# Cross-attention kernel: the weighted sum accumulates in one PSUM bank, two banks by turns, and its division and rounding change engines

## The reference, cut to what matters

```
scores = einsum(Q, K) * scale          # per sentence: 16 heads x 56 queries = 896 rows, 1500 keys
attn   = softmax(scores)
out    = einsum(attn, V)               # the weighted sum
x      = x + out.reshape(...) @ Wo
```

## Time and profile before

| | |
|---|---|
| median of 3 runs | 4035.7 us (4034.22 to 4037.05) |
| the profiled execution, its own time | 4029.83 us |
| its span, first to last instruction | 4028.0 us |
| mean granted TensorE clock | 0.954 of full speed |
| VectorE / ScalarE / GpSimd busy | 78% / 66% / 63% |
| matmuls | 43467 |

### The profile page before, as it was taken

The page is one execution under the profiler, slowest core; times in us unless marked ns, Lnnn a source line. Parts: engine busy times, 40 slices in busy tenths (PEclk is TensorE's granted clock), DMA queues, the critical chain, the costliest instruction groups (busy, mean ns, idle before and its releaser), DMA issues.

```text
span 4028.0 us, 110585 instructions
## 1 busy us (share of the span) xinstructions
PE 3794.2 (94%) x43467; PEld 2887.3 (72%) x43467; DVE 3136.7 (78%) x6499; ACT 2673.5 (66%) x5365; POOL 2545.3 (63%) x2457
## 2 busy tenths in 40 slices
PE   6999999989979999999799999996997899999987
PEld 4777777766647777777577777775665677777765
DVE  6999999858888888887688887886654788888864
ACT  4887887756647777777377777772542577777752
POOL 4888888759856766677466766664001476676761
PEclk8999999979989999999699999997998899999998
DMA  5333333125432221221122122110000212222100
GB/s 130 104 110 111 112 107 109 41 90 159 142 111 57 60 61 54 60 61 43 28 60 61 54 61 61 54 56 19 3 1 18 65 54 64 57 58 63 55 22 15
DMA packets 157328, 266.80 MB, mean 66 GB/s; under 512 B 26632, under 2 KB 97432, under 8 KB 155432
## 3 DMA queue, kind: packets, MB, share of 16 engines
q1 hardware_dynamic: 156360, 259.67, 22.6%
q10 hardware_dynamic: 448, 0.06, 0.0%
HBM read 165.10 MB, written 50.26 MB: 53 GB/s over the span
## 4 chain that ended last, share of the span: by engine, by line
PE 87%; DVE 6%; POOL 2%; ACT 2%; DMA 1%; issue 1%; SPq 1%; POOLq 0%; DVEq 0%; ACTq 0%
PE ps L186 83%; PE ps L665 1%; DVE xn L166 1%; POOL wst L545 1%; PE ps L242 1%; DVE wst L823 1%; PE ps L255 1%; PE ps L1639 1%; DMA big<-big 1%; PE ps L1161 0%; DVE st L151 0%; DVE wst L778 0%; DVE relu L775 0%; ACT wb L324 0%; PE ps L193 0%
## 5 line engine op out<-in xcount | busy, mean ns | idle before, releaser
L545 POOL TENSOR_TENSOR wst<-wst 125x384 bf16<-125x384 f32 (+1 forms) x1536 | 1432.2, 932 | 833.1 <-ACT wst L751 772.3
L751 ACT ACTIVATE wst<-ps 125x448 f32<-125x448 f32 x3072 | 1518.1, 553 | 568.3 <-PE ps L186 553.8
L186 PE MATMUL ps<-big,cx 128*125 128x448 bf16 (+1 forms) x6144 | 1427.4, 353 | 0.7 <-DMA big<-topT 0.7
L186 PEld LDWEIGHTS ps<-cx,wst 125*128 125x128 bf16 x23040 | 1113.6, 98 | 307.5 <-POOL wst L545 15.2
L823 DVE TENSOR_TENSOR wst<-wst 125x512 bf16<-125x512 f32 (+1 forms) x1536 | 1270.2, 827 | 56.7 <-ACT wst L751 56.5
L186 PE MATMUL ps<-cx,wst 125*128 125x65 bf16 (+2 forms) x23040 | 1202.4, 204 | 12.1 <-POOL wst L545 11.6
L186 PEld LDWEIGHTS ps<-big,cx 128*125 128x125 bf16 (+1 forms) x6144 | 834.5, 137 | 283.9 <-issue 1.8
L186 PE MATMUL ps<-cx,big 128*128 128x500 bf16 (+1 forms) x2688 | 709.8, 317 | 10.2 <-DVE big L1744 2.6
L778 DVE TENSOR_REDUCE wst<-ps 128x1 f32<-128x500 f32 x896 | 604.5, 675 | 136.3 <-PE ps L186 123.6
L775 DVE CUSTOM_DVE_ANT_0 wst<-ps,wst 128x500 bf16<-128x500 f32 x448 | 302.9, 676 | 195.0 <-PE ps L186 150.5
L775 DVE CUSTOM_DVE_ANT_0 relu<-ps,relu 128x500 bf16<-128x500 f32 x448 | 302.1, 674 | 149.7 <-PE ps L186 81.4
(11 more groups left out here) (250 smaller groups left out, 4213.2 us busy)
## 6 DMA issues: line engine op xcount, KB each, us to landing
big<-big SPq DMA_DIRECT2D x768, 56.0 KB, 2.7
cx<-ctxT SPq DMA_DIRECT2D x96, 375.0 KB, 3.5
cx<-ctxN SPq DMA_DIRECT2D x64, 377.9 KB
cx<-in_ctxN SPq DMA_DIRECT2D x64, 375.0 KB
cx<-ctxT SPq DMA_DIRECT2D x96, 187.5 KB, 3.8
ctxN<-cx SPq DMA_DIRECT2D x32, 377.9 KB
ynN<-cx SPq DMA_DIRECT2D x32, 377.9 KB
cx<-ynN SPq DMA_DIRECT2D x32, 377.9 KB
```

What stands on the lines that cost most here:

```text
L186: return t.matmul(o, l, r, start=start, stop=stop, skip_group_check=True)
L545: g.tensor_tensor(pl[r][0:KP, at:], pf[r][0:KP, at:], pf[r][0:KP, at:].bitcast(BF16)[:, 1::2], ALU.subtract).then_inc(s["plp"], 1)
L751: e.activation(pf[T % 3][0:KP, cols], bank(2 + n2 % 3, 448)[0:KP], ACT.Exp, scale=scale).then_inc(s["ev"], 1)
```

## The change

The accumulator becomes one bank: the high weights times the low values are a matmul of their own that adds into the first 64 of a block's 65 columns. So a sentence needs 7 x 65 = 455 columns, and two banks (5 and 6) are used by turns. A step has 21 matmuls (7 x 65, 64, 65 columns). VectorE takes the reciprocal and multiplies straight out of PSUM into `raw`, ScalarE rounds from `raw` into `O`, and GpSimd only subtracts; the stage's last subtraction is VectorE's. TensorE waits for the accumulator of two sentences ago.

```diff
-        raw = [wst[:, 4032 + 903 * i:4935 + 903 * i].rearrange("p (j c) -> p j c", j=NJ) for i in range(2)]
+        raw = [wst[:, 4032 + 448 * i:4480 + 448 * i].rearrange("p (j c) -> p j c", j=NJ) for i in range(2)]
+        acc = [bank(5 + i, 65 * NJ) for i in range(2)]
...
# pool_cross
-                if 0 <= (k := due(T, KT + 4)) < B - 1:
-                    w.wait_ge(s["fc"], 2 * (kb + 1))
-                    g.tensor_tensor(r, r, raw[u][:, :, C + 1:], ALU.add).then_inc(s["fp"], 1)
...
-                if 0 <= (k := due(T, KT + 7)) < B - 1:
-                    w.wait_ge(s["rd"], kb + 1)
-                    g.tensor_tensor(r, r, per_row(rden[u][:, :], C), ALU.mult).then_inc(s["fp"], 1)
...
-                if 0 <= (k := due(T, KT + 8)) < B - 1:
-                    g.tensor_copy(O[:, k % HB, :, 0:C], r).then_inc(s["fp"], 1)
...
-                if 0 <= (k := due(T, KT + 10)) < B - 1:
-                    g.tensor_tensor(O[:, k % HB, :, C:], r, O[:, k % HB, :, 0:C], ALU.subtract).then_inc(s["fp"], 1)
+                if 0 <= (k := due(T, KT + 6)) < B - 1:
+                    kb = B * ci + k
+                    w.wait_ge(s["fp"], 2 * kb + 1)
+                    g.tensor_tensor(O[:, k % HB, :, C:], raw[k % 2], O[:, k % HB, :, 0:C], ALU.subtract).then_inc(s["fp"], 1)
+                    w.wait_ge(s["fp"], 2 * kb + 2)
+
+        def pe_values(t, w, ci, T):
+            k, i = divmod(T, KT)
+            r, kb = T % 3, B * ci + k
+            ph, o, of = pf[r][0:KP, :].bitcast(BF16)[:, 1::2], acc[k % 2], cnb[k % 3]
+            w.wait_ge(s["pl"], NT * ci + T + 1)
+            wait_values(w, ci, k)
+            if kb >= 2:
+                w.wait_ge(s["fc"], kb - 1)
+            for j in range(NJ):
+                if j == JP[ci]:
+                    w.wait_ge(s["plp"], NT * ci + T + 1)
+                cols, at = slice(128 * j, 128 * j + 128), 65 * j
+                mm(t, o[:, at:at + 65], ph[:, cols], of[:, i, 0:65], i == 0 and j == 0, False)
+                mm(t, o[:, at:at + 64], ph[:, cols], of[:, i, 65:129], False, False)
+                n = mm(t, o[:, at:at + 65], pl[r][0:KP, cols], of[:, i, 0:65], False, i == KT - 1)
+            n.then_inc(s["pv"], 1)
+
+        def dve_values(v, w, ci, k):
+            u, kb = k % 2, B * ci + k
+            o = acc[u].rearrange("p (j c) -> p j c", j=NJ)
+            w.wait_ge(s["pv"], KT * (kb + 1))
+            v.reciprocal(rden[u][:, :], o[:, :, C]).then_inc(s["rd"], 1)
+            if k >= 2:
+                w.wait_ge(s["fp"], 2 * (kb - 1))
+            w.wait_ge(s["rd"], kb + 1)
+            v.tensor_tensor(raw[u], o[:, :, 0:C], per_row(rden[u][:, :], C), ALU.mult).then_inc(s["fc"], 1)
+            if k == B - 1:
+                w.wait_ge(s["fp"], 2 * kb + 1)
+                v.tensor_tensor(O[:, k % HB, :, C:], raw[u], O[:, k % HB, :, 0:C], ALU.subtract).then_inc(s["fp"], 1)
+
+        def act_values(e, w, ci, k):
+            kb = B * ci + k
+            w.wait_ge(s["fc"], kb + 1)
+            w.wait_ge(s["fp"], 2 * kb)
+            if k >= HB:
+                w.wait_ge(s["otr"], kb - HB + 1)
+            e.activation(O[:, k % HB, :, 0:C], raw[k % 2], ACT.Copy).then_inc(s["fp"], 1)
...
# pe_cross: L634 to L653 become
+                    pe_values(t, w, ci, T - 2)
...
# act_cross: L724 to L731 become
+                if (k := due(T, KT + 4)) >= 0:
+                    act_values(e, w, ci, k)
...
# dve_cross: L800 to L815 go; after the subtraction of L823
+                if (k := due(T, KT + 2)) >= 0:
+                    dve_values(v, w, ci, k)
```

More of the change, by code:

```diff
@@ L547, in pool_cross @@
                     w.wait_ge(s["plp"], NT * ci + T)
-                if 0 <= (k := due(T, KT + 4)) < B - 1:
-                    u, kb = k % 2, B * ci + k
-                    r = raw[u][:, :, 0:C]
-                    w.wait_ge(s["fc"], 2 * (kb + 1))
-                    g.tensor_tensor(r, r, raw[u][:, :, C + 1:], ALU.add).then_inc(s["fp"], 1)
-                    w.wait_ge(s["fp"], 4 * kb + 1)
-                if 0 <= (k := due(T, KT + 7)) < B - 1:
-                    u, kb = k % 2, B * ci + k
-                    r = raw[u][:, :, 0:C]
-                    w.wait_ge(s["rd"], kb + 1)
-                    g.tensor_tensor(r, r, per_row(rden[u][:, :], C), ALU.mult).then_inc(s["fp"], 1)
-                    w.wait_ge(s["fp"], 4 * kb + 2)
@@ L560, in pool_cross @@
-                if 0 <= (k := due(T, KT + 8)) < B - 1:
[L561 to L564, removed]
-                    g.tensor_copy(O[:, k % HB, :, 0:C], r).then_inc(s["fp"], 1)
-                    w.wait_ge(s["fp"], 4 * kb + 3)
-                if 0 <= (k := due(T, KT + 10)) < B - 1:
-                    u, kb = k % 2, B * ci + k
-                    r = raw[u][:, :, 0:C]
-                    g.tensor_tensor(O[:, k % HB, :, C:], r, O[:, k % HB, :, 0:C], ALU.subtract).then_inc(s["fp"], 1)
-                    w.wait_ge(s["fp"], 4 * kb + 4)
+                if 0 <= (k := due(T, KT + 6)) < B - 1:
[3 more added lines that the diff above has]
+                    w.wait_ge(s["fp"], 2 * kb + 2)
@@ L662, in pe_cross @@
                 if what == "turn":
-                    w.wait_ge(s["fp"], 4 * (b0 + k + 1))
+                    w.wait_ge(s["fp"], 2 * (b0 + k + 1))
                     for j in range(NJ):
@@ L799, in dve_cross @@
                     v.tensor_reduce(top[k % 2][:, 0:NJ], mx[k % 2], AX.X, ALU.max, negate=True).then_inc(s["nmx"], 1)
[L800 to L815, removed]
                 for k, items in turns(T):
```

## The result

| | before | changed |
|---|---|---|
| median (4 runs each, same chip) | 4034.96 us | 4054.99 us (4052.28 to 4057.07) |
| ratio, 95% interval | | 1.0047 [1.0031, 1.0063] |
| profiled execution, own time | 4029.83 us | 4052.28 us |
| its span | 4028.0 us | 4050.5 us |
| mean granted TensorE clock | 0.954 | 0.96 |

The changed kernel is 20 us slower by the medians, half a per cent with the interval clear of 1, and 22.5 us by the two profiled spans. From here on, "a period" is the time between the starts of two weighted blocks 24 steps apart (median over a stage), and "a block" the time from the start of a step's weighted block to the start of what follows it.

A forecast was written before the change was run, and what follows sets the result against it. TensorE, busy 94% of the span, bounds the kernel; +33 for added matmuls, -13 for waits and -5.4 for stage ends give +14.6 us, from 4029.8 to 4044 profiled, 4050 for the median, range 4014 to 4080.

The forecast's parts named there:

- The bound: Steady part of a stage: TensorE streams columns plus a small price per matmul, 46.04 us per 24 steps, without stalling.
- Part one: Weighted block: six more matmuls a step at 3.6 ns each, 21.4 ns a step, +33 us, with no cover.
- the stated upper bound of 5.8: Added matmuls priced at 5.8 ns each, like the four score matmuls: 35 ns a step, +53 us.
- Part two: Stage ends: TensorE's loads wait less for GpSimd's L545; 13 of 15.2 us go, bounds 8 and 15.2.
- Part three: Stage end, last sum to transposes: 3.71 us becomes 2.36, giving back 1.35 a stage, 5.4 in all.
- Part four: Load on other engines: VectorE gains a 0.63 us product a sentence, L552's going returns 0.3 us; net nothing.
- rival 4: VectorE becomes late: its product falls wholly on TensorE's path each sentence, 81 us more, 4130; chance 0.05.
- The sum: Whole kernel: +33 - 13 - 5.4 = +14.6 us, 4044 for the profiled execution, 4050 for the median.
- Rival 1: Weighted block: added matmuls nearly free, 2.5 ns for all 21, growth under 12 ns a step; -15 us, 4020; chance 0.27.
- Rival 2: In between: 1.2 to 2.9 ns for each added matmul, a result within 8 us of 4036; chance 0.18.
- Rival 5: Weight loads set the pace: 41 ns a pair, +0.25 us a step, 378 us, 4410; chance 0.02.
- the clock's gain: Stage ends: clock staying up over the shorter gap speeds transposes and output matmuls, up to 9 us; not counted in forecast.

The follow-up runs named there:

- experiment 1: Kernel before with only the matmuls split (65 and 64 columns, 21 a step), accumulator, copies and GpSimd's jobs kept; 4069.01 against 4034.73 us, ratio 1.0085.
- experiment 4: Changed kernel with all 21 matmuls of a step on the dense low weights, high weights left out of the sum; 4055.13 us in one run.
- experiment 3: Changed kernel with the three matmuls reordered: high 65, low 65, high 64; 4060.23 us in one run.
- experiment 5: Changed kernel with the 64-wide matmul reading columns 0 to 63 of `cnb` instead of 65 to 128; 4045.17 us in one run.
- experiment 6: Changed kernel without its 64-wide matmuls, so 14 of 65 columns a step; 3817.11 us in one run against 4035.61 for the kernel before.
- experiment 2: Kernel before with its 15 matmuls, but VectorE multiplies in SBUF, ScalarE rounds, GpSimd keeps two of four jobs; 4034.49 against 4034.73 us, ratio 1.0.
- experiment 8: Kernel before with the multiplying moved to VectorE and rounding to ScalarE in stages two to four only; 4027.94 against 4035.61 us, ratio 0.9981.
- experiment 9: Kernel before with matmuls split into 64 and 65 columns in six of seven blocks, 65 and 64 in the other; 4075.75 against 4033.0 us.
- experiment 10: Kernel before with six added one-column matmuls a step, with their weight loads, into columns nothing reads; 4255.84 against 4033.0 us, one run each.
- experiment 7: Changed kernel with VectorE's product out of PSUM done twice per sentence; 4126.96 us against 4035.61 for the kernel before, ratio 1.0226.

## Why the prediction was right

The sign, the mechanism and the time, 4050 against 4055, hold. By its steps:

- **The bound.** Confirmed: TensorE's period is the chain in both kernels, and experiment 1 shows that the matmuls alone carry the steady loss.
- **Part one, the added matmuls: mis-sized.** They were taken at the period's average, 3.6 ns, +33 us; measured 4.7 ns, 9216 x 4.7 = +43 us, between the average and the stated upper bound of 5.8. The reason given for the choice, the stride of the high weights, is wrong (experiment 4). The step that failed is that an average over 594 unlike matmuls was taken for the added kind. The 5.8 itself came of rounded starts: single starts give that row of four score matmuls 764 ns (1441.185 to 1441.949), which is also the median of all such groups in stage two, and so (764 - 746.7) / 4 = 4.3 ns. The dearest kind of those rows is then the products of 500 columns, 213.4 ns from start to start for 208.3 ns of columns, and the upper bound by them would have been +47 us and not +53. The trace of before held a nearer row: block 3, which crosses the bank boundary, already was cut into 65 and 64 columns. There the next matmul starts 30.9 and 33.0 ns behind the two pieces, 63.8 in all, against 57.7 behind one of 129, so the split could be priced at about 6 ns. By the 2.5 ns of the Trainium skill (TensorE: Matmul & The Clock Gate, Back-to-back issue gap) the estimate would have been +23 us; that is the price of the 56-wide matmuls but not of these.
- **Part two, the waits.** They fell from 15.2 to 0.8 us, -14.4; predicted -13. All of them had lain in the last 30 to 40 us of the stages, as argued from the earlier trace rows.
- **Part three, the stage's end.** It went from 3.71 to 2.40 us, -5.2 over four stages; predicted 2.36 and -5.4. TensorE's gap before the transposes shrank from 3.36 to 2.05 us, the clock stayed full over it, and the transposes run 0.35 us shorter, another -1.4. Of the output matmuls' 1.8 us a stage only 0.7 us came in all four together: the clock fell between the end of the transposes and the first of these matmuls, or within 0.4 us of it. In between TensorE waits 1.01 us for the transposes' copy, a second gap that the prediction didn't look at. How far the clock's part rests on the shorter gap is open. In the kernels of experiments 3 to 6, with the same gap, the clock was full over all seven transposes at 8 of 16 stage ends; with the old gap (before and experiments 1, 2, 8, 9, 10) at 1 of 24.
- **Part four, VectorE.** The product is free in stages two to four (46.72 with it, 46.73 without, in stage three 47.13 and 47.14), as said. The 0.3 us that were to come back from L552 don't show there: the mean of the 512-wide L823 was 779 ns before and its successor's 782. Still, TensorE's loads wait for VectorE only 0.7 us in all from 1216 to 1905 us. In stage one it cost 3.5 us, which uses up what the longer block would have hidden of the waits that VectorE already caused there (experiment 1's stage one grew by 0.49 us a period, not 0.68; the changed kernel's by 0.71). The stage had no row of its own in the prediction, though it is the one with `JP` = 5. And "8.6 us idle" was a weaker argument than it looked: experiment 7 shows that a second 0.63 us would have cost 72 us, close to rival 4's 81.
- **The sum.** +43.3 - 14.4 - 5.2 - 1.4 - 0.7 = +21.6, against +22.5 by the spans. The predicted +14.6 was short by the 10 of part one, of which some 3 came back in parts two and three. That the median came out only 5 us off is luck to that extent; it also rose by only 20 us where the profiled execution rose by 22.5.
- **The rivals.** Rival 1 needed less than 12 ns a step; it was 30. Rival 2 ended at 2.9 ns for each added matmul; it was 4.7. Rival 4 holds in no stage but the first, with 3.5 us. Rival 5 (41 ns a pair) fell: an added pair costs 31.4 ns. The low end of the range has a slip: rival 1 with half of the clock's gain is 4020 - 4.5 = 4016, not 4014.

What would have shown it was 46.5 for the period and 0.637 for the block; they came out at 46.72 and 0.646, under the 46.8 that was set as the mark of a wrong forecast.

## What to carry to other kernels

Where TensorE's starts show that it streams without a gap, count the matmuls as well as the columns: cutting one in two cost 4.7 ns here, and an added one with its load never less than 25 in all, so a layout that needs fewer PSUM banks at the price of more matmuls has to earn it elsewhere. Look first whether the kernel already holds one of the kind that will be added, and take its price from single starts, not from rounded ones. Relief of a side engine is worth only the waits that end on it (here the last two sentences of each stage); give it by moving that work alone, as experiment 8 does, and leave it out in the stage where the receiving engine is fuller. Before calling an engine's idle time room, look where in the sentence it lies, or double the moved work and see.

## What was not expected of the hardware

- The price of a matmul beyond its columns at full clock, from its start to the next one's, depends on its kind: 2.1 to 2.5 ns (65 columns, low weights), 2.7 (56), 4.0 (129), 4.3 (448, mean of both kinds), 4 to 5 (500), 6.1 (64, from column 65 of its operand). Stride of the weights, order of the loads and the place of the accumulator don't change it; what the moving operand reads does, by 3.1 ns on the matmul itself, of which 1.1 to 1.4 are left once the others have slowed (experiment 5). Its cause is open.
- A one-column matmul with its load takes 25 ns.
- The same 448-column product on VectorE takes 0.62 to 0.63 us out of PSUM in all 128 cases, though GpSimd is at work beside 127 of them. Out of SBUF it takes 0.61 to 1.24 us: 1.00 in the mean of stage one in experiment 2, 0.64 in that of stages two to four in experiment 8. GpSimd is at work beside the quick ones too, so which of its operations delays it is open.
- Over a gap of TensorE of 2.05 us the granted clock stayed full at some stage ends and fell at others, and once it stayed full over one of 3.36 us (stage one of experiment 2).
